# New orders for the five queues at both ends of a two-layer graph kernel: beta's products with W2 behind the first product with W

## The reference

```
A_hat = adj + I;  d = rowsum(A_hat)^-1/2
h0 = relu(layernorm(x))
x1 = x + (d A_hat d) (h0 W + b)                      # layer 0

xh = relu(layernorm(x1))                             # layer 1
H  = (adj != 0);  w = first row of adj
P  = H diag(1/colcount(H)) H^T;  Dn = 1/(H w)
h  = relu(Dn * P (xh W1^T) + b1)                     # 128 x 1024
hn = layernorm(h) * gamma + beta
out = x1 + xh + Dn * P (hn W2^T) + b2
```

## Time and profile before

| what | value |
|---|---|
| median of 3 runs | 1989.92 us (1989.72 to 1991.07) |
| the profiled execution's own time | 1990.53 us |
| its span | 1988.7 us |
| PE busy | 1956.6 us, 98% |
| DVE, POOL, ACT busy | 1724.4, 1246.7, 1091.4 us |
| chain that ended last | PE 96%, DVE 1%, issue 1%, DMA 1% |
| loaded and stored | 48.24 MB read, 33.55 MB written |

### The profile page before, as it was taken

How to read it: one execution, slowest core, us unless ns; L and a number is a source line. 1 busy time by engine, 2 the same in 40 slices (tenths; PEclk the granted TensorE clock), 3 DMA queues, 4 the chain that set the end, 5 groups by cost and what they waited for, 6 DMA issues and landing times.

```text
span 1988.7 us, 42836 instructions
## 1 busy us (share of the span) xinstructions
PE 1956.6 (98%) x10390; PEld 949.8 (48%) x10390; DVE 1724.4 (87%) x4514; ACT 1091.4 (55%) x2099; POOL 1246.7 (63%) x1934
## 2 busy tenths in 40 slices
PE   5999999999999999999999999999999999999998
PEld 2444444444444444444444444444444444444443
DVE  7898888888888888888888888888888888888885
ACT  7555555555555555555555555555555555555553
POOL 4566666666666666666666666666666666666553
PEclk9999999999999999999999999999999999999999
DMA  5344334333433443343343334334433433433432
GB/s 179 78 94 101 86 87 93 95 86 89 102 86 87 93 95 86 89 102 86 87 93 95 86 88 101 86 87 94 95 86 88 100 86 87 94 95 86 88 78 67
DMA packets 467951, 182.90 MB, mean 92 GB/s; under 512 B 416336, under 2 KB 432720, under 8 KB 467920
## 3 DMA queue, kind: packets, MB, share of 16 engines
q1 hardware_dynamic: 467920, 182.55, 40.1%
HBM read 48.24 MB, written 33.55 MB: 41 GB/s over the span
## 4 chain that ended last, share of the span: by engine, by line
PE 96%; DVE 1%; issue 1%; DMA 1%; ACT 0%; POOL 0%; SPq 0%; DVEq 0%; POOLq 0%; ACTq 0%
PE ps_c L405 33%; PE ps_u L405 33%; PE ps_e L405 16%; PE ps_e L428 1%; PE ps_c L394 1%; PE ps_c L393 1%; PE ps_c L392 1%; PE ps_e L430 1%; PE ps_e L429 1%; PE ps_y L428 1%; PE ps_y L430 1%; PE ps_y L429 1%; PE ps_a L463 1%; PE ps_p L471 0%; PE ps_p L472 0%
## 5 line engine op out<-in xcount | busy, mean ns | idle before, releaser
L579 ACT ACTIVATE h<-z 128x512 f32<-128x512 f32 x256 | 160.9, 629 | 535.0 <-DVE z L785 534.9
L1181 POOL TENSOR_TENSOR rd<-u,neg_half 128x2 f32<-128x2 f32 x128 | 178.9, 1398 | 231.7 <-DVE y L1001 224.4
L405 PE MATMUL ps_c<-w1h,t1h 128*128 128x512 f16 x1024 | 263.7, 380 | 1.5 <-DVE t1l L945 0.9
L405 PE MATMUL ps_c<-w1l,t1h 128*128 128x512 f16 x1024 | 263.1, 379 | 0.0
L405 PE MATMUL ps_c<-w1h,t1l 128*128 128x512 f16 x1024 | 262.8, 379 | 0.0
L405 PE MATMUL ps_u<-w2h,hnT_hi 128*128 128x512 f16 x1024 | 243.6, 381 | 2.2 <-DMA hnT_hi<-hn_hi 2.2
L405 PE MATMUL ps_u<-w2l,hnT_hi 128*128 128x512 f16 x1024 | 242.0, 379 | 0.0
L405 PE MATMUL ps_u<-w2h,hnT_lo 128*128 128x512 f16 x1024 | 241.9, 379 | 0.0
L1227 POOL TENSOR_TENSOR scr<-x1b,xh 128x512 f32<-128x512 f32 x128 | 231.1, 1806 | 1.0 <-ACT xh L620 0.7
L1162 POOL TENSOR_TENSOR base<-scr,vq 128x512 f32<-128x512 f32 x128 | 224.1, 1751 | 9.3 <-ACT vq L573 5.9
L1001 DVE SCALAR_TENSOR_TENSOR y<-b_sc,rd,ps_e 128x512 f32<-128x512 f32 x128 | 95.6, 747 | 142.7 <-PE ps_e L405 142.7
(11 more groups left out here) (125 smaller groups left out, 4423.2 us busy)
## 6 DMA issues: line engine op xcount, KB each, us to landing
x_t<-in_x_dram SPq DMA_DIRECT2D x128, 256.0 KB, 2.7
out_dram<-out_t SPq DMA_DIRECT2D x128, 256.0 KB, 2.2
adj_t<-in_adj_dram SPq DMA_DIRECT2D x128, 64.0 KB, 2.3
raw_w<-in_W1T_dram SPq DMA_DIRECT2D x4, 512.0 KB, 6.9
raw_w<-in_W2T_dram SPq DMA_DIRECT2D x8, 256.0 KB, 7.7
h0T_hi<-h_hi SPq DMA_TRANSPOSE x128, 2.4
h0T_lo<-h_lo SPq DMA_TRANSPOSE x128, 2.4
hnT_hi<-hn_hi SPq DMA_TRANSPOSE x128, 3.1
```

The costliest lines, as they stand in the source:

```text
L405: mm = pe.matmul(ps, t[:, j * 128:(j + 1) * 128], w[:, j, cols], start=(n == 0 and j == 0), stop=(n == 2 and j == blocks - 1))
L579: act.activation(h[:, cols], z[:, cols], ACT.Relu).then_inc(s_h[n], 1)
L1181: pool.tensor_tensor(rd0[:, m, :], u0[:, m, :], neg_half[:, :], ALU.pow).then_inc(s_pp0, 1)
```

## The change

Only the orders written out ahead of the loop and behind it change, on PE, ACT, DVE and POOL at both ends and on SP ahead of the loop. The set of steps is the same; `step`, the loop, is untouched. In the head:

- SP issues one block of W1T first, then adj(1), adj(0), blocks of W with x(0) between; b, gamma and beta later. W2T's blocks stand between and behind the transpositions of graph 0 and 1; b2 and b1 behind those of graph 1.
- PE: weight_sum(1) and the second and third do_AT stand as before, but do_Y0(0) comes right behind, with do_P(1) and do_AT(3); all eight blocks of beta come after it, around do_Z0(0), weight_sum(2) and do_Y0(1), and before do_T1(0).
- ACT squares W1T's first block ahead of W, and b after W; h0(0) and h0_hi(0) come ahead of the last squares; the four splits of W stand together; W2's squares all come before W1T's last two splits.
- DVE: the statistics of graph 0 come before the scale of W; do_HB_lo(1) behind do_h0_lo(1); the splits of W together.
- POOL: the scalars of graph 0 ahead of W's power.

In `do_cm` (DVE) a wait for the step before's inverse is added, outside the loop alone. In the tail the orders are shuffled; do_Y2(NG - 3) moves ahead of do_U(NG - 2), do_out(NG - 3) ahead of do_hn(NG - 1).

The diff, cut to its core (lines that go are shown for SP, PE and ACT; where DVE's and POOL's go, the lines stand in the kernel above):

```diff
@@ -342,35 +342,36 @@
                 do_ldX(k + 4, i)
                 do_ldA(k + 4, i)
 
+            load_weight(1, raw_w1, W1T, range(0, 1))
+            load_adj(1)
+            load_adj(0)
+            load_weight(0, raw_w0, W, range(1, 2))
+            load_x(0)
+            load_weight(0, raw_w0, W, range(0, 1))
+            load_gamma_beta()
+            load_weight(0, raw_w0, W, range(2, 4))
             load_row(b_all, b, s_b)
-            load_weight(0, raw_w0, W, range(0, 3))
-            load_adj(0)
-            load_weight(0, raw_w0, W, range(3, 4))
-            load_weight(1, raw_w1, W1T, range(0, 2))
-            load_adj(1)
+            load_weight(1, raw_w1, W1T, range(1, 4))
+            load_x(1)
             load_adj(2)
-            load_x(0)
-            load_weight(1, raw_w1, W1T, range(2, 4))
-            load_weight(2, raw_w2, W2T, range(1, 2))
-            load_x(1)
+            do_tr0h(0)
+            load_x(2)
+            do_ldA(4); do_tr0l(0); do_ldA(5)
+            load_weight(2, raw_w2, W2T, range(0, 3))
             load_adj(3)
+            load_x(3)
+            load_weight(2, raw_w2, W2T, range(4, 5))
+            do_ldA(6)
             load_weight(2, raw_w2, W2T, range(3, 4))
-            load_gamma_beta()
-            load_weight(2, raw_w2, W2T, range(0, 1))
-            load_weight(2, raw_w2, W2T, range(2, 3))
-            load_weight(2, raw_w2, W2T, range(5, 6))
-            load_x(3)
-            load_x(2)
-            do_tr0h(0); do_tr0l(0); do_ldA(4)
+            load_weight(2, raw_w2, W2T, range(5, 7))
+            do_tr0h(1); do_tr0l(1)
             load_weight(2, raw_w2, W2T, range(7, 8))
-            load_weight(2, raw_w2, W2T, range(6, 7))
-            load_weight(2, raw_w2, W2T, range(4, 5))
             load_row(b2_all, b2, s_rows)
             load_row(b1_all, b1, s_rows)
-            do_tr0h(1); do_ldA(5); do_tr0l(1); do_ldX(4); do_tr0h(2); do_ldA(6); do_tr0l(2); do_trh(0)
-            do_trl(0); do_tr0l(3); do_ldX(5); do_tr0h(3); do_ldA(7); do_ldX(6); do_trh(1); do_trl(1); do_st(0)
-            do_ldX(7); do_tr0l(4); do_ldA(8); do_tr0h(4); do_tr0h(5); do_tr0l(5); do_trl(2); do_ldX(8)
-            do_trh(2); do_trh(3); do_trl(3); do_ldA(9); do_st(1); do_tr0l(6); do_tr0h(6); do_ldX(9)
+            do_ldX(4); do_tr0h(2); do_tr0l(2); do_ldX(5); do_trh(0); do_trl(0); do_tr0h(3); do_ldA(7)
+            do_tr0l(3); do_trh(1); do_trl(1); do_ldA(8); do_tr0h(4); do_ldX(6); do_ldX(7); do_tr0l(4)
+            do_st(0); do_tr0l(5); do_tr0h(5); do_trh(2); do_trl(2); do_ldA(9); do_ldX(8); do_trh(3); do_trl(3)
+            do_tr0h(6); do_tr0l(6); do_st(1); do_ldX(9)
             steady(sp, ENG.SP, step)
             do_tr0h(NG - 5); do_trh(NG - 8); do_trl(NG - 8); do_tr0l(NG - 5); do_st(NG - 10); do_ldX(NG - 2)
...
@@ -516,33 +517,34 @@
                 do_Y1b(k - 1, i)
                 do_U(k - 2, i)
 
-            do_AT(0)
+            do_AT(0); do_AT(1); do_P(0)
             weight_sum(0, slice(0, KI + 1))
-            do_P(0); do_AT(1); do_AT(2)
+            do_AT(2)
             weight_sum(1, slice(KI + 1, 2 * KI + 1))
+            do_Y0(0); do_P(1); do_AT(3)
             beta_row(range(0, 2))
-            do_Y0(0); do_AT(3)
+            do_Z0(0)
             beta_row(range(2, 4))
-            do_Z0(0); do_P(1)
+            weight_sum(2, slice(2 * KI + 1, 2 * KI + 1 + KH))
             beta_row(range(4, 6))
-            weight_sum(2, slice(2 * KI + 1, 2 * KI + 1 + KH))
-            do_Y0(1); do_T1(0)
+            do_Y0(1)
             beta_row(range(6, 8)).then_inc(s_vps, 1)
-            do_Y1a(0); do_Z0(1); do_Y1b(0); do_Y0(2); do_T1(1); do_P(2); do_Z0(2); do_AT(4); do_Y1b(1)
-            do_Y1a(1); do_U(0); do_T1(2); do_Y0(3); do_Y1b(2); do_Y2(0); do_Z0(3); do_Y1a(2); do_P(3)
-            do_AT(5); do_U(1); do_T1(3); do_Y0(4); do_Y2(1); do_P(4); do_Y1b(3); do_Z0(4); do_Y1a(3); do_AT(6)
-            do_Y0(5); do_U(2); do_T1(4); do_Z0(5); do_P(5); do_AT(7); do_Y2(2); do_Y1b(4); do_Y1a(4); do_U(3)
+            do_T1(0); do_Z0(1); do_Y1a(0); do_Y1b(0); do_Y0(2); do_T1(1); do_AT(4); do_P(2); do_Z0(2)
+            do_Y1b(1); do_Y1a(1); do_U(0); do_T1(2); do_Y0(3); do_P(3); do_AT(5); do_Y1b(2); do_Z0(3)
+            do_Y1a(2); do_Y2(0); do_AT(6); do_U(1); do_P(4); do_T1(3); do_Y0(4); do_Y1a(3); do_Z0(4)
+            do_Y1b(3); do_Y0(5); do_Y2(1); do_U(2); do_T1(4); do_Z0(5); do_AT(7); do_P(5); do_Y2(2); do_Y1b(4)
+            do_Y1a(4); do_U(3)
             steady(pe, ENG.PE, step)
-            do_T1(NG - 7); do_Y0(NG - 6); do_Y2(NG - 9); do_Y1b(NG - 7); do_P(NG - 6); do_AT(NG - 4)
...
+            do_T1(NG - 3); do_Y0(NG - 2); do_P(NG - 2); do_Y1a(NG - 3); do_Y2(NG - 5); do_Z0(NG - 2)
             do_Y1b(NG - 3); do_U(NG - 4); do_T1(NG - 2); do_Y0(NG - 1); do_P(NG - 1); do_Y1a(NG - 2)
             do_Z0(NG - 1); do_Y1b(NG - 2); do_U(NG - 3); do_T1(NG - 1); do_Y2(NG - 4); do_Y1a(NG - 1)
-            do_Y1b(NG - 1); do_U(NG - 2); do_Y2(NG - 3); do_Y2(NG - 2); do_U(NG - 1); do_Y2(NG - 1)
+            do_Y1b(NG - 1); do_Y2(NG - 3); do_U(NG - 2); do_Y2(NG - 2); do_U(NG - 1); do_Y2(NG - 1)
 
...
@@ -681,69 +683,60 @@
                 do_vq(k - 1, i)
                 do_P_hi(k + 1, i)
 
+            do_rsum(0)
+            square_sum(1, raw_w1, w1h, range(0, 1))
+            do_rsum(1); do_A_hi(0)
+            square_sum(0, raw_w0, w0h, range(0, 3))
+            do_h0(0); do_P_hi(0); do_h0_hi(0); do_A_hi(1)
+            square_sum(0, raw_w0, w0h, range(3, 4))
             square_sum_b()
-            square_sum(0, raw_w0, w0h, range(0, 4))
-            do_A_hi(0); do_rsum(0)
-            square_sum(1, raw_w1, w1h, range(0, 1))
-            do_P_hi(0)
-            square_sum(1, raw_w1, w1h, range(1, 2))
-            split_hi(0, raw_w0, w0h, range(0, 1))
-            do_rsum(1)
-            split_hi(0, raw_w0, w0h, range(1, 2))
-            square_sum(1, raw_w1, w1h, range(2, 3))
-            do_A_hi(1)
-            square_sum(1, raw_w1, w1h, range(3, 4))
-            do_h0_hi(0)
-            split_hi(0, raw_w0, w0h, range(2, 3))
-            do_h0(0)
+            square_sum(1, raw_w1, w1h, range(1, 4))
+            do_rsum(2)
+            split_hi(0, raw_w0, w0h, range(0, 4))
+            split_hi(1, raw_w1, w1h, range(0, 1))
             square_sum(2, raw_w2, w2h, range(0, 1))
-            do_rsum(2)
-            split_hi(1, raw_w1, w1h, range(0, 1))
-            split_hi(0, raw_w0, w0h, range(3, 4))
-            split_hi(1, raw_w1, w1h, range(1, 2))
+            do_h0(1)
             square_sum(2, raw_w2, w2h, range(1, 2))
             do_h0_hi(1)
-            split_hi(1, raw_w1, w1h, range(2, 3))
-            do_h0(1)
             square_sum(2, raw_w2, w2h, range(2, 3))
+            split_hi(1, raw_w1, w1h, range(1, 2))
+            square_sum(2, raw_w2, w2h, range(3, 4))
             do_yh(0)
-            square_sum(2, raw_w2, w2h, range(3, 8))
-            split_hi(1, raw_w1, w1h, range(3, 4))
-            do_xh(0); do_xh_hi(0); do_P_hi(1); do_rsum(3); do_A_hi(2)
+            square_sum(2, raw_w2, w2h, range(4, 5))
+            do_A_hi(2)
+            square_sum(2, raw_w2, w2h, range(5, 8))
+            split_hi(1, raw_w1, w1h, range(2, 4))
+            do_rsum(3); do_P_hi(1); do_xh(0); do_h0_hi(2); do_xh_hi(0); do_rsum(4); do_yh(1)
             split_hi(2, raw_w2, w2h, range(0, 1))
             do_t1h(0)
             split_hi(2, raw_w2, w2h, range(1, 2))
-            do_h0_hi(2); do_yh(1)
-            split_hi(2, raw_w2, w2h, range(2, 3))
             do_h0(2)
-            split_hi(2, raw_w2, w2h, range(3, 4))
-            do_ha(0)
-            split_hi(2, raw_w2, w2h, range(4, 6))
-            do_rsum(4)
+            split_hi(2, raw_w2, w2h, range(2, 6))
+            do_h0_hi(3)
             split_hi(2, raw_w2, w2h, range(6, 7))
-            do_xh(1); do_hb(0); do_xh_hi(1); do_h0(3); do_yh(2); do_t1h(1); do_h0_hi(3); do_hn_hi(0); do_vq(0)
-            do_A_hi(3); do_P_hi(2)
+            do_xh(1); do_ha(0); do_hb(0); do_xh_hi(1); do_A_hi(3)
             split_hi(2, raw_w2, w2h, range(7, 8))
-            do_rsum(5); do_xh(2); do_hb(1); do_xh_hi(2); do_rsum(6); do_ha(1); do_t1h(2); do_uh(0); do_h0(4)
-            do_hn_hi(1); do_yh(3); do_h0_hi(4); do_vq(1); do_A_hi(4); do_rsum(7); do_P_hi(3); do_ha(2)
-            do_xh(3); do_xh_hi(3); do_hb(2); do_t1h(3); do_uh(1); do_h0(5); do_A_hi(5); do_h0_hi(5); do_yh(4)
-            do_hn_hi(2); do_P_hi(4); do_vq(2); do_hb(3); do_ha(3); do_xh(4); do_xh_hi(4); do_A_hi(6); do_yh(5)
-            do_hn_hi(3); do_uh(2); do_t1h(4); do_P_hi(5); do_h0_hi(6); do_h0(6); do_rsum(8); do_vq(3)
-            do_rsum(9); do_hb(4); do_A_hi(7); do_ha(4); do_xh(5); do_xh_hi(5); do_h0_hi(7); do_vq(4); do_uh(3)
-            do_t1h(5); do_hn_hi(4); do_h0(7); do_yh(6); do_P_hi(6)
+            do_h0(3); do_yh(2); do_t1h(1); do_hn_hi(0); do_rsum(5); do_P_hi(2); do_vq(0); do_hb(1); do_xh(2)
```

(61 more changed lines are left out.)

196 lines of the change are left out of this document (69 added, 127 removed).

## The result

The changed kernel takes **1994.12 us** (median; 1991.92 to 1996.41) beside 1990.47 us (1989.26 to 1992.80) of the kernel before: ratio 1.0019, 95% interval 1.0013 to 1.0025. It is slower, by 3.65 us. The forecast was 1986.3 us, with 1982.5 to 1990.5 as its range.

What follows compares the result with a forecast made beforehand. PE was taken as fully busy mid-kernel, leaving 32 us of idle at the ends plus lower-clock stretches. Span 1988.7 minus 3.6 (head) minus 0 (tail) gave 1985.1, or 1986.3 us at the median; range 1982.5 to 1990.5.

Steps and rivals of the forecast that it cites:

- Part 4, the tail: Behind the loop: the last chain from Y1b(127) to the last U stays; effect 0, bounds -1.5 and +1.0 us.
- Part 1, loads and Y0(0): Kernel start: reordered loads at 383 KB per us start h0(0)'s chain 4 us sooner; Y0(0) ends at 22.9 or 23.7.
- Part 2: Head, beta's products behind Y0(0): new wait of 1.4 to 2.2 us at P(1), nothing gained up to Y1a(0).
- the term of the first beta pair: Head, first two beta blocks behind P(1): taken at full clock, 1.9 us, from 25.4 to 27.3.
- rival (a): Head: PE stays at 1.2 GHz, first beta pair costs 3.78, Z0(0) at 29.2; 1988.1 us; chance 0.17.
- Rival (c): Head: P(1) blocks PE's queue, late h0_hi(1) delays everything; 1990.8 us, 1992.7 with the lower clock; chance 0.10.
- Part 3: Y1a(0) to the loop: U(0) 3.2 us sooner, 1.0 more from later idle, 0.6 charged for POOL; head gains 3.6.
- Rival (d): Head: the change does no more than swap, the walk being optimistic by what it gains; 1989.5 us; chance 0.10.

Runs made afterwards that it cites:

- half-change kernels: The change cut at the loop: old orders up to it and new behind, 1992.98 us, +2.9; new up to it and old behind, 1989.39 us, -0.7.
- the other heads: New orders up to the loop, old behind, with further edits: P(1) early 1988.64 us, b's load first 1989.83, shortened chain 1987.97, that with b first 1988.39.
- the run with the old tail: New orders up to the loop, the old ones behind it, on all five queues: 1989.39 us, -0.7 against the kernel before, ratio 0.9996.
- 128 pads: The changed kernel with 128 tiny writes of VectorE ahead of its first operation: 1994.80 us, +5.0 against the kernel before, ratio 1.0024.
- 24 pads: The changed kernel with 24 tiny writes (128x1) of VectorE ahead of its first operation: 1991.97 us, +2.2 against the kernel before, ratio 1.0012.

## Why the prediction was wrong

**Part 4, the tail, is the step that failed.** It was put at 0 with bounds -1.5 and +1.0. The half-change kernels put the new tail at +2.9 (with the old head) and 3.65 + 0.7 = 4.3 us (with the new). The walk looked at the last chain alone, from Y1b(127) to U(127), and that did stay: 0.86 before Y1a(127), 1.49 before Y2(126), 0.93 before U(127), beside 0.86, 2.14 and 0.74 in the earlier trace rows, where the 0.65 us that Y2(125) was to take from the second are gone as forecast. It took for granted that what lies before that chain runs without a wait because it did before. Between 1896 and 1911 it doesn't, and the material to see it was in the trace of before: DVE's one wait on "issue", 1.99 us. I never asked what the new order puts behind a pause that is tied to the code. The lower bound was built from the waits that PE showed in the tail before (0.69 and 0.86 us), the upper one, +1.0, from no row at all; neither bounds a new wait.

**Part 1, loads and Y0(0): right in the main.** The first transposition of adj ran at 5.09 us (forecast 6.3), Y0(0) from 18.72 to 24.1 (forecast end 22.9, or 23.7 at the lower clock). The load rate was not steady: 103 GB/s from 8 to 10 us, where the sum had 383. ACT's last square of W1T ended at 17.7 (forecast 17.2).

**Part 2: the term of the first beta pair was mis-sized.** P(1)'s wait is 2.16 us (forecast 1.4 to 2.2). The pair behind it took 3.62 us, not 1.9:

```profile
22.88 1.22 PE L406 MATMUL ps_e<-w0h,h0T_lo 128*128 128x512 f16 x4
26.26 0.22 PE L472 MATMUL ps_p<-HB_w,H_T 128*128 128x130 f16 x1 [2.16 <-DVE HB_w L823]
26.31 0.22 PE L473 MATMUL ps_p<-HB_lo,H_T 128*128 128x128 f16 x1
26.49 0.30 PE L464 MATMUL ps_a<-ident,adj_t 128*128 128x128 f32 x1
26.72 3.62 PE L424 MATMUL ps_y<-raw_w,bet_wide 128*128 128x512 f32 x4
30.18 0.38 PE L429 MATMUL ps_e<-yh,A_hi 128*128 128x512 f16 x1
```

That is rival (a), with the pair near its price of 3.78; Z0(0) came at 30.2, where the rival had 29.2 and the sum 27.7. The clock by stretch (PE, weight loads, DVE, ACT, POOL, clock, DMA share, GB/s):

```profile
23.00:26.70 3.70, 1.54 (x8) 0.51 (x7) 3.70 (x16) 3.70 (x8) 0.00 (x0) 0.99 0.71 225
26.70:30.10 3.40, 3.40 (x5) 1.31 (x5) 2.91 (x6) 3.00 (x10) 0.70 (x1) 0.50 0.72 180
```

The way there was another than the rival's first half: PE was at the higher clock by the end of Y0(0) (four matmuls in 1.22 us at 22.88) and fell to 0.50 behind the wait. The earlier trace rows had held a warning: behind the wait of 2.20 us before T1(1) the four matmuls at 51.99 took 1.91, while the prediction named only the wait of 1.75 that did not lower the clock. The traces of the other heads go with the wait in front of the pair: 3.29 us behind a wait of 2.48 and 3.58 behind 2.19, but 1.95 behind 1.21, 1.40 and 1.55. The Trainium skill (TensorE: Matmul & The Clock Gate, "Part 1: The HAM clock gate") says that activity releases the throttle; the slow pair agrees with the rival drawn from it, though the scattered Y0(0) itself, by the row at 22.88, had released it. Rival (c)'s mechanism, P(1) blocking PE's queue, was there too; my chain missed that P(1) also waits for dn(0), which ended after HB_lo(1).

**Part 3: the direction of the chain failed, its end is another than forecast.** The rows that answer to the earlier trace rows:

```profile
39.87 0.22 PE L393 MATMUL ps_c<-P_hi,xh_hi 128*128 128x128 f16 x1 [0.92 <-issue]
...
51.94 0.22 PE L393 MATMUL ps_c<-P_hi,xh_hi 128*128 128x128 f16 x1 [1.70 <-issue]
...
55.53 1.91 PE L406 MATMUL ps_c<-w1h,t1h 128*128 128x512 f16 x4
...
61.63 1.67 PE L406 MATMUL ps_u<-w2h,hnT_hi 128*128 128x512 f16 x7
```

Each step comes later than forecast: T1(0) at 39.87 (forecast 37.0), T1(1) at 51.94 (47.2), and the half clock behind it, which the sum struck out as a gain of 1.2 us, is still there (1.91 us for four matmuls). U(0) is 3.25 us later than before where 3.2 sooner was forecast. Yet in the loop the same matmuls run only 0.5 us later (113.06 against 112.53 for a Y0 of its first turns), mostly because the 2.38 us of idle from 60 to 110 are gone altogether: the sum had credited 1.0 for them. The two errors partly cancel, by luck: by the run with the old tail the head is worth 0.7 us, which its interval can't tell from nothing, instead of 3.6. Rival (d), a head that only swaps, is what the head did (its 1989.5 is 0.4 under the 1989.92 that such a head gives).

Of the 7.8 us between forecast and median (1986.3 and 1994.12), some 3 are the head's and some 4 the tail's; 0.5 is the level of the runs (1989.92 against 1990.47). The measured 0.19% lies just inside what the prediction called the same, with a chance of 0.53, but above the stated range and above rival (c) at its full price, 1992.7; the chance of 0.09 for slower by over 0.2% was put on the head's walk alone.

## What to carry to other kernels

Behind a hardware loop with straight code after it, look at each engine's own timeline for an idle time on "issue", and count which operations stand behind it: a reorder moves work across that pause even where it leaves the critical chain alone. The pause goes by the count of instructions, the waiting ones too. Comparing two orders of a queue, test them with some idle operations at the start of the queue; here that alone put the changed kernel anywhere from +0.4 to +5.0 us beside before, more than either half of the change. And a bound on "no new wait" can't be built from the waits that the old trace shows.

## What the runs showed of the hardware

- **An engine waits for its code.** VectorE stood still for 1.4 to 3.8 us once behind the loop in all sixteen traces, with a transfer of 8 KB on an instruction queue that started in the pause (0.6 us ahead of it where the pause was 1.4); from the start of that transfer to the next instruction it was 1.7 to 2.1 us every time. The place is fixed by the number of instructions ahead of it: 829 or 831 in fourteen traces, 957 = 829 + 128 with 128 pads, 822 in the kernel before, each the first step of 128 behind the loop. The transfers in the changed kernel's head are in step with it: they start with 73, 200, 325, 451 and 580 rows of VectorE behind them. In the changed kernel ScalarE and GpSimd show one such stall each (1.83 and 1.97 us), with a transfer of the same queue in it, which no wait of TensorE names. The Trainium skill (Advanced Engine Details and Errata, "ISA Cache") gives lines of 16 KB, 256 instructions, two of them in 32 KB (128 KB on TensorE), and says that the size can be configured per engine; for VectorE the runs here show blocks of 8 KB and 128 instructions, and the measurement decides. Why the stall lasts 1.4 us in one kernel and 3.8 in another stays open.
- **A semaphore instruction takes up code like any other.** Between w_hi(125) and HB_hi(124) stand 11 operations and 11 instructions that only wait, and 24 pads moved the stall by these 22 rows.
- **The same waits don't always lower the clock.** Waits of 1.72 and 1.90 us left it at 0.51 from 1904 to 1911, and 1.70 and 2.04 left 0.50 from 1908 to 1910; 0.84 and 2.26 left it at 1.00, and so did 1.57 and 1.98 in the one trace with 24 pads. At the end of the kernel before, 2.14 and 0.74 us stood ahead of the slow U(127). Neither the length nor the number of the waits tells these apart.
- **A row broadcast to 128 partitions loads slowly**: the two us that hold b's 256 KB show 103 GB/s in the changed kernel and 147 with b first (103 to 222 over the traces with the new load order), beside some 300 to 400 in the stretches around.
